# A router's mask and row weights moved from VectorE to GpSimd in a recurrence plus mixture-of-experts kernel

## The reference

```
d = sigmoid(x Wd + bd);  i = x Wi + bi;  h_t = d_t * h_(t-1) + i_t       # recurrence over the tokens
x = layernorm(x + (layernorm(h) * gamma + beta) + x)

gate = x Wg^T + routing_bias                                              # 8 experts
mask = the 4 largest of 8 (ties: the lower index first)
weights = softmax(gate where mask) * mask
ffn(u; w1, w2, w3) = (silu(u w1) * (u w2)) w3                             # hidden size 682
x = layernorm(x + ffn(x; shared) + sum over the 4 chosen experts of weight * ffn(x; expert))
```

## Time and profile before

| | us |
|---|---|
| three runs | 982.51, 984.04, 985.51 (median 984.04) |
| profiled execution | 981.17 |
| its span | 979.4 |
| PE busy | 960.3 (98%) |
| PEld busy | 785.1 (80%) |
| DVE busy | 560.8 (57%) |
| POOL busy | 554.8 (57%) |
| ACT busy | 504.7 (52%) |

### The profile page before, as it was taken

How to read it: one execution, slowest core, us unless ns; L and a number is a source line. 1 busy time by engine, 2 the same in 40 slices (tenths; PEclk the granted TensorE clock), 3 DMA queues, 4 the chain that set the end, 5 groups by cost and what they waited for, 6 DMA issues and landing times.

```text
span 979.4 us, 25637 instructions
## 1 busy us (share of the span) xinstructions
PE 960.3 (98%) x8131; PEld 785.1 (80%) x8131; DVE 560.8 (57%) x1410; ACT 504.7 (52%) x1259; POOL 554.8 (57%) x547
## 2 busy tenths in 40 slices
PE   9997999999999999999999999999999999999997
PEld 4554667788887888888788878788888887887885
DVE  4899977745554446544545445444454454544686
ACT  3666544445554455545455445444555554554366
POOL 4586047759433348534855035086898870885883
PEclk9999999999999999999999999999999999999999
DMA  6887124473532333533345214129754881795785
GB/s 224 248 167 172 28 70 125 101 212 101 160 104 89 98 100 94 158 109 101 92 103 135 59 39 145 46 54 198 119 94 85 125 123 49 110 131 88 101 153 143
DMA packets 168052, 113.88 MB, mean 116 GB/s; under 512 B 113596, under 2 KB 160191, under 8 KB 166848
## 3 DMA queue, kind: packets, MB, share of 16 engines
q0 software_dynamic: 29808, 58.37, 27.2%
q1 hardware_dynamic: 115888, 33.15, 16.8%
q10 hardware_dynamic: 22304, 21.76, 6.7%
HBM read 47.09 MB, written 43.12 MB: 92 GB/s over the span
## 4 chain that ended last, share of the span: by engine, by line
PE 80%; POOL 6%; DVE 5%; issue 3%; DMA 3%; ACT 1%; SPq 1%; ACTq 0%; DVEq 0%; POOLq 0%
PE psA L1161 50%; PE psB L1192 21%; PE psA L1090 5%; POOL y_sum L805 3%; DMA rows_by_place<-y_rows,place 2%; POOL rows_by_place L741 2%; PE psB L1195 2%; PE psA L1192 1%; DVE g_lo L1614 1%; PE psB L1103 1%; PE psC L1134 1%; DVE work L1380 0%; DMA y_sum<-rows_by_place,place 0%; DVE g L1604 0%; PE psC L1263 0%
## 5 line engine op out<-in xcount | busy, mean ns | idle before, releaser
L913 ACT ACTIVATE sil<-psA 128x256 f32<-128x256 f32 (+1 forms) x456 | 178.6, 399 | 273.8 <-PE psA L1161 237.1
L805 POOL DMA_INDIRECT y_sum<-rows_by_place,place x128 | 199.5, 1558 | 81.2 <-issue 37.8
L1604 DVE SCALAR_TENSOR_TENSOR g<-psA,sil 128x256 f32<-128x256 f32 (+1 forms) x160 | 71.9, 450 | 297.2 <-ACT sil L913 296.6
L1161 PE MATMUL psA<-xb_odd,work 128*128 128x256 f16 x1980 | 221.1, 273 | 0.2 <-issue 0.2
L1161 PEld LDWEIGHTS psA<-xb_odd,work 128*128 128x128 f16 x1980 | 193.5, 98 | 23.0 <-issue 0.6
L1192 PE MATMUL psB<-work,g_hi 128*128 128x256 f16 x1260 | 211.1, 273 | 0.0
L1161 PE MATMUL psA<-xb,work 128*128 128x256 f16 x1782 | 199.0, 273 | 2.2 <-issue 1.2
L1161 PEld LDWEIGHTS psA<-xb,work 128*128 128x128 f16 x1782 | 173.8, 98 | 24.0 <-issue 4.0
L1604 DVE SCALAR_TENSOR_TENSOR psC<-psA,sil 128x256 f32<-128x256 f32 (+3 forms) x296 | 133.0, 449 | 77.8 <-ACT sil L913 72.3
L752 POOL DMA_INDIRECT rows_by_place<-y_rows,place x96 | 95.0, 989 | 136.6 <-DMA rows_by_place<-y_rows,place 121.2
L1192 PE MATMUL psB<-work,g_lo 128*128 128x256 f16 x630 | 171.7, 273 | 0.0
(11 more groups left out here) (191 smaller groups left out, 1010.7 us busy)
## 6 DMA issues: line engine op xcount, KB each, us to landing
stage<-wpack POOLq DMA_DIRECT2D x9, 2176.0 KB, 9.1
rows_by_place<-eb ACTq DMA_DIRECT2D x57, 256.0 KB
work<-xT SPq DMA_DIRECT2D x7, 512.0 KB, 6.1
work<-half_beta SPq DMA_DIRECT2D x6, 512.0 KB, 5.7
work<-x_tok POOLq DMA_DIRECT2D x6, 512.0 KB, 6.0
rows_by_place<-eb ACTq DMA_DIRECT2D x6, 384.0 KB
rows_by_place<-zeros SPq DMA_DIRECT2D x1, 2112.0 KB, 13.5
rows_by_place<-y_rows,place POOLq DMA_INDIRECT x128, 2.5
```

The source lines that it names most:

```text
L805: pool.indirect_dma_start(out=y_sum[:, n, :], out_offset=None, in_=xs, in_offset=bass.IndirectOffsetOnAxis(ap=place[:, k, n:n + 1], axis=0 ...
L913: act.activation(sil[r0:r0 + n, c % SLOTS, 0:T], psA[0:n, chunk_bank(c, T), 0:T], ACT.Silu, scale=1.0 / (XS * WS)).then_inc(silu_ready, 1)
L1161: last = pe.matmul(dst, W[:, ws, k, ci, :], xb[slot][:, KD * xs_ + k, 0:T], start=(k == 0 and n == 0), stop=(k == KD - 1 and n == 2))
L1604: dve.scalar_tensor_tensor(gated_rows(g, c, 0, n, T), src, 1.0 / (XS * WS), sil[r0:r0 + n, c % SLOTS, 0:T], ALU.mult, ALU.mult).then_inc(g ...
```

## The change

It does these things:

- **Mask on POOL** (`choose`): difference of each logit from the fourth largest, of the four largest from it, equality and greater-than, running counts of the equal ones by three additions (ties), and from these the mask; in all sixteen operations behind the maxima, the first of which is the shift for the exponentials. DVE keeps the 32 maxima, now all behind the last logits, between the products of chunks 4 and 5 of block 0.
- **Row weights on POOL** (`weigh`): multiplication by the mask, sum of 8 in three additions, power of -0.5, square, scale, product.
- **Exponentials** on ACT ahead of block 1 instead of after it; the last step's normalisation goes beside the chunks of block 1.
- **Order on DVE**: low parts of rows beside chunks 1 and 2 of block 1, counts beside 3, place keys beside 4, half the key maxima beside 5 and half at the block's end. PE's rank product stands after chunk 2.
- **Order on PE** in the recurrence: states of the next step ahead of the second half of the products.
- **SP**: the zero fill is issued in step 6 instead of step 1.
- **PE's loop over pairs** is written out four times, with fixed pair words and constant waits.
- Two memsets of constants fall away.

```diff
@@ sync @@
-                if s == 1:
-                    fill_spare()
                 if s == EARLY - 2:
                     load_ahead(0)
+                if s == EARLY:
+                    fill_spare()
@@ gpsimd @@
+            def choose():
+                t = Tally(pool, route_steps)
+                fourth = top[:, :, K - 1:K]
+                equal, pair_sum, quad_sum = ties
+                pool.wait_ge(y_ready, NSTEP - 1)
+                for tie in ties:
+                    t.add(pool.memset(tie[:, :, 0:K], 0.0))
+                pool.wait_ge(largest_ready, 1)
+                pool.tensor_tensor(ex[:, :, :], gate[:, :, :], top[:, :, 0:1].to_broadcast([P, NT, E]), ALU.subtract)\
+                    .then_inc(shifted_ready, 1)
+                t.add(pool.tensor_tensor(over, gate[:, :, :], fourth.to_broadcast([P, NT, E]), ALU.subtract))
+                t.add(pool.tensor_tensor(fours, top[:, :, 0:K], fourth.to_broadcast([P, NT, K]), ALU.subtract))
+                t.wait()
+                t.add(pool.tensor_scalar(equal[:, :, K:TW], over, 0.0, 1.0, ALU.is_equal, ALU.mult))
+                t.add(pool.tensor_scalar(fours, fours, 0.0, 1.0, ALU.is_equal, ALU.mult))
+                t.wait()
+                t.add(pool.tensor_scalar(over, over, 0.0, 1.0, ALU.is_gt, ALU.mult))
+                t.add(pool.tensor_tensor(pair_sum[:, :, K:TW], equal[:, :, K:TW], equal[:, :, K - 1:TW - 1], ALU.add))
+                t.add(pool.tensor_tensor(twos, fours[:, :, 0:2], fours[:, :, 2:4], ALU.add))
+                t.wait()
+                t.add(pool.tensor_tensor(quad_sum[:, :, K:TW], pair_sum[:, :, K:TW], pair_sum[:, :, K - 2:TW - 2],
+                                         ALU.add))
+                t.add(pool.tensor_tensor(fours[:, :, 0:1], twos[:, :, 0:1], twos[:, :, 1:2], ALU.add))
+                t.wait()
+                t.add(pool.tensor_tensor(tie_rank, quad_sum[:, :, K:TW], quad_sum[:, :, 0:E], ALU.add))
+                t.wait()
+                t.add(pool.tensor_tensor(tie_rank, fours[:, :, 0:1].to_broadcast([P, NT, E]), tie_rank, ALU.subtract))
+                t.wait()
+                t.add(pool.tensor_scalar(tie_rank, tie_rank, 0.0, 1.0, ALU.is_ge, ALU.mult))
+                t.wait()
+                t.add(pool.tensor_tensor(tie_rank, tie_rank, equal[:, :, K:TW], ALU.mult))
+                t.wait()
+                pool.tensor_tensor(mask_h[:, :, :], tie_rank, over, ALU.add).then_inc(mask_ready, 1)
+            def weigh():
+                ...
+                t.add(pool.tensor_tensor(es_root[:, :], es[:, :], neg_half[:, 0:1].to_broadcast([P, NT]), ALU.pow))
+                ...
             pool.wait_ge(rows_marked, 8)
+            choose()
+            weigh()
@@ scalar @@
-            normed(NSTEP - 1)
+            act.wait_ge(shifted_ready, 1)
+            act.activation(ex[:, :, :], ex[:, :, :], ACT.Exp).then_inc(exps_ready, 1)
+            act.activation(nstat[0][:, 0, 0:2], bd, ACT.Silu).then_inc(table_loaded, 1)
+            act.wait_ge(table_loaded, 1)
...
-            ffn_block(1, TL)
-            act.wait_ge(shifted_ready, 1)
...
+            ffn_block(1, TL, beside=lambda c: normed_part(NSTEP - 1, c))
@@ tensor @@
                 turn_parts(s)
-                if s + AHEAD < NSTEP:
-                    products(s + AHEAD, [1])
...
                 if s + 1 < NSTEP:
                     states(s + 1)
+                if s + AHEAD < NSTEP:
+                    products(s + AHEAD, [1])
+                if s + 1 < NSTEP:
                     gate_sums(s + 1)
...
-            ffn_block(SH, 1, TL, early_slot(1), beside=lambda c: ranks() if c == 3 else None)
+            ffn_block(SH, 1, TL, early_slot(1), beside=lambda c: ranks() if c == 2 else None)
...
-            with pe.Fori(0, E // 2) as p:
-                counted(pe, weight_set_ready, 2 * p + 1)
-                expert_turns(0, lambda c: read_second(pair_words[0], c))
...
+            for p in range(E // 2):
+                pe.wait_ge(weight_set_ready, 2 * p + 1)
+                expert_turns(0, lambda c: read_second(pair_words[p], c))
+                pe.wait_ge(weight_set_ready, 2 * p + 2)
+                expert_turns(1, lambda c: read_first(pair_words[p + 1], c) if p + 1 < E // 2 else None)
@@ vector @@
             low_first(1)
             gated_first(3)
-            largest_early()
             low_first(2)
             gated_first(4)
+            largest()
             low_first(3)
             gated_first(5)
             low_first(4)
             low_first(5)
-            choose(0, EARLY_CHOSEN)
```

More of the change, by code:

```diff
@@ L166, in build @@
         seg = sb("seg", [P, E, NT], F32)
-        tot, inc = (work[:, 11, n * NT * E:(n + 1) * NT * E].rearrange("p (e t) -> p e t", e=E) for n in range(2))
-        key = work[:, 11, 2 * NT * E:3 * NT * E].rearrange("p (t e) -> p t e", e=E)
+        tot, inc = (work[:, 12, n * NT * E:(n + 1) * NT * E].rearrange("p (e t) -> p e t", e=E) for n in range(2))
+        key, over = (work[:, 12, n * NT * E:(n + 1) * NT * E].rearrange("p (t e) -> p t e", e=E) for n in (2, 3))
+        TW = K + E
+        ties = [work[:, w, n * NT * TW:(n + 1) * NT * TW].rearrange("p (t e) -> p t e", e=TW)
+                for w, n in ((10, 0), (10, 1), (12, 0))]
+        tie_rank = work[:, 12, NT * TW:NT * (TW + E)].rearrange("p (t e) -> p t e", e=E)
+        fours = work[:, 10, 2 * NT * TW:2 * NT * TW + NT * K].rearrange("p (t e) -> p t e", e=K)
+        twos = work[:, 10, 2 * NT * TW + NT * K:2 * NT * TW + NT * (K + 2)].rearrange("p (t e) -> p t e", e=2)
         place = sb("place", [P, K, NT], U32)
@@ L866, in acts, with normed_part, normed @@
                         .then_inc(products_read, 1)
-            def normed(s):
+            def normed_part(s, part):
                 b = s % B
                 g0 = tok(s) // P
-                act.wait_ge(rstd2_ready, s + 1)
-                for j in range(JT):
-                    last = act.activation(y[:, g0 + j, :], zr[b][:, j, :], ACT.Identity,
-                                          scale=rs2[b][:, j:j + 1], bias=nb2[b][:, j:j + 1])
-                last.then_inc(y_ready, 1)
-                act.wait_ge(y_ready, s + 1)
-                act.activation(y_hl[:, g0:g0 + JT, 0, :], y[:, g0:g0 + JT, :], ACT.Copy, scale=XS)\
-                    .then_inc(y_high_ready, 1)
+                if part == 0:
+                    act.wait_ge(rstd2_ready, s + 1)
+                if part < JT:
+                    last = act.activation(y[:, g0 + part, :], zr[b][:, part, :], ACT.Identity,
+                                          scale=rs2[b][:, part:part + 1], bias=nb2[b][:, part:part + 1])
+                    if part == JT - 1:
+                        last.then_inc(y_ready, 1)
+                else:
+                    act.wait_ge(y_ready, s + 1)
+                    act.activation(y_hl[:, g0:g0 + JT, 0, :], y[:, g0:g0 + JT, :], ACT.Copy, scale=XS)\
+                        .then_inc(y_high_ready, 1)
+            def normed(s):
+                for part in range(JT + 1):
+                    normed_part(s, part)
             def copy_sums(s):
@@ L995, in first_high @@
                     .then_inc(first_high_ready, 1)
-            ffn_block(1, TL)
-            act.wait_ge(shifted_ready, 1)
-            act.activation(ex[:, :, :], ex[:, :, :], ACT.Exp).then_inc(exps_ready, 1)
-            act.activation(nstat[0][:, 0, 0:2], bd, ACT.Silu).then_inc(table_loaded, 1)
-            act.wait_ge(table_loaded, 1)
+            ffn_block(1, TL, beside=lambda c: normed_part(NSTEP - 1, c))
             def first_high_beside(g):
@@ L1725, in _ @@
             low_first(5)
-            choose(0, EARLY_CHOSEN)
-            t.wait()
-            t = late
             add_shared(0, ahead_tiles(0))
```

109 lines of the change are left out of this document (37 added, 72 removed).

## The result

The changed kernel takes 988.9 us, median of 9 runs (987.46 to 995.08), the kernel before 984.04 (981.58 to 986.73, 9 runs on the same chip): ratio 1.0051, 95% interval 1.0031 to 1.0071. That is +4.9 us, where +2.1 was forecast; 988.9 lies above the forecast's own range (983.5 to 988.5) and inside the whole one (980 to 990). "Slower by over 0.3%" had a chance of 0.33.

A forecast was written before the change was run, and what follows sets the result against it. PE bounds the experts, so its arrival there sets the end. Recurrence -2.8, blocks 0 and 1 +6.0, pairs -0.8, hand-over -0.3 sum to +2.1 us: 986.1 on the median, own range 983.5 to 988.5, whole 980 to 990.

The forecast's parts named there:

- What bounds the kernel: PE is busy 687.73 of 690 us from 200 to 890, so whatever moves its arrival at the experts moves the end.
- Recurrence, -2.8: Steps 1 and 3: DVE's waits of 1.98 and 1.46 us shrink by PE's order and the later fill; -1.3 to -3.4.
- Blocks 0 and 1, +6.0: Late maxima, the mask on POOL and DVE's longer list at block 1's end hold PE: +6.0 us.
- three of the second (1.2): In the mask on POOL: three 256-element operations with one input, 0.41 us each, within an undisturbed 9.0 us.
- +3.2 of block 0: Block 0's down projection on PE ends at 106.7 instead of 103.47, held by late low parts and POOL's turns.
- Pairs, -0.8: Entry to the second pair of experts: written out, PE is spared the loop's return, 0.82 us of issue.
- Hand-over, -0.3: At the first expert PE's wait of 0.31 us for rows goes, as PE comes later than the rows.
- weights on POOL hold the port: Block 1's end: a 5.2 us power on POOL blocks DVE's counts' scan, 3.5 more, +5.6 in all, 989.6; chance 0.27.
- the port costs nothing: Blocks 0 and 1: the mask is in time, only DVE's list at block 1's end holds PE; -1.1, 982.9; chance 0.15.
- PE is not held at all: Blocks 0 and 1: low parts and mask come in time, so only gains are left, 979.8; chance 0.21.

The follow-up runs named there:

- fill_between: The kernel before with PE's new recurrence order and the zero fill behind the eighth norm and the loads of block 1's rows: 982.88 us, ratio 0.9980.
- pairs_loop: The changed kernel with PE's counted loop over the pairs put back: 987.17 us, ratio 1.0038 to the kernel before.
- pairs_only: The kernel before with only PE's four pairs of experts written out instead of a loop: 987.23 us, ratio 1.0033.
- maxima_last: pairs_loop with DVE's maxima behind block 0's last low part, rank products, counts and keys moved back with them: 987.04 us, ratio 1.0028 to the kernel before.
- keys_in_block2: pairs_loop with the place keys at block 1's end and both halves of their maxima in block 2: 986.24 us, ratio 1.0016 to the kernel before.

## Why the prediction was right, and where it was not

- **What bounds the kernel**: right. PE from 200 to 890 is busy 686.05 of 690 (before 687.73), and what moves its arrival moves the end, but for what the phase takes or gives. That making the router's way shorter "is worth 0.3 us at most" held only while PE was no earlier: 2.9 us earlier it is worth 2.05 (fill_between).
- **Recurrence, -2.8**: right as a size (-2.93, -2.94, -2.87, -2.92 in four kernels), but not in every run of the kernel as it stands. "It shares the engines with step 7's x, asked for some 10 us after its issue: 0 to +1, I take 0" failed: it is step 6's x that POOL asks for at the moment of the fill, and in the two traces where they meet within 0.6 us the price is 5.1. Most runs of the changed kernel seem to be spared it: -2.9, +5.5, +3.3 and -0.3 make +5.6 (an estimate from the kernels above), near the +4.9 of the median, while with the wait it would be some +10.8. The order alone gave +0.12: it needs the fill out of its way.
- **Blocks 0 and 1, +6.0**: right in size, 5.48 to 5.71 in the four kernels that have these edits, and right in its path (late maxima, late mask, then the lists at block 1's end), but partly by luck. The maxima, which follow the last logits (forecast near 97) at once, start at 98.25 in pairs_loop, 97.15 on before's clock. Block 0's down projection waits 2.24 (3.2), the rank product 1.83 in the changed kernel (1.9). The mask itself, 12.4 forecast and 11.55 measured, came out by two errors against each other: "three of the second (1.2)" are comparisons and take 1.10, 1.08 and 1.08 undisturbed, so that the undisturbed mask is about 10.7 instead of 9.0, and the disturbance by DVE is some 0.8 instead of 3.4. The +3.2 of block 0 is no cost of its own either: the wait for the mask holds PE to the same moment.
- **Pairs, -0.8**: the failed step. Alone the edit costs +3.3 (+1.1 to +5.3), and undoing it in the changed kernel moves the ratio from 1.0051 to 1.0038, with overlapping intervals. I had "0 if new code must be fetched as slowly" as the worst end; the wait is 2.25 to 2.32 in three kernels, against 0.67 to 0.82 with the loop. The term is off by 4.1 us alone and by some 2 in the changed kernel; the gap between forecast and result is 2.8. The Trainium skill, in "Runtime: NRT & Kernel Launch", section "Instruction fetch mechanics", says that a branch taken out of the window makes an engine fetch before it goes on, and that kernels therefore prefer unrolling; here the loop's turn cost less than entering new code. The instruction queue moved 0.59 MB in place of 0.33; that the wait is for this fetch is likely and not shown, since the profile names no releaser for it.
- **Hand-over, -0.3**: right, no wait at the first expert.
- **Rival "weights on POOL hold the port"**: its price was right (5.45 for 5.2), its consequence refuted: DVE's two-input operations ran at their usual length inside it. The rule that I had cited for it, in the Trainium skill's "SBUF — State Buffer", section "SBUF: two separate sides" (the one that starts first keeps the pair for its whole instruction), fits the 1.53 us subtractions as far as a low part that starts inside one goes, not the power; the trace decides.
- **Rival "the port costs nothing"**: refuted by the stretched low parts and mask operations, but nearer than I had it: the price on PE's path is about the 0.8 us by which the mask is later (an estimate). That the mask would be "there before PE asks" with the port free was wrong by the comparisons: at 10.7 us it ends near 113, where 111.45 was asked.
- **Rival "PE is not held at all"** did not come true, but the order for it exists: it decides where the maxima, the rank products and the counts stand, not three us earlier logits, as I had put it.
- **Not foreseen**: the experts' 0 to 2.9 us by phase.

Open stay why a transfer that starts 0.6 us before the fill is delayed by 5 us and one 1.6 us before not at all, and the rest of pairs_only's loss.

## What to carry to other kernels

Moving work off an engine that is not the bound wins nothing where it stood in cover; what counts is which instruction is now first in line behind a late input. Put the operation that waits for another engine behind everything the bound is waiting for, and the product that consumes it as late as its consumer allows. A wait of the bound engine costs nothing of its own when a later wait would have held it to the same moment; price the chain that ends last, not each wait. Before timing small edits ahead of a long steady stage, look whether that stage has a beat between two engines: its phase can hide or fake 0.3%.

## What the runs showed of the hardware

- After its 5.52 us wait (90.38) PE was granted half its clock, and the 36 matmuls behind it took 8.19 us (36 of the same take 6.01 at 103.17 in fill_between, at full clock). The windows of the changed kernel (start:end, length, busy by engine, clock, DMA share, GB/s):

```profile
88.00:94.00 6.00, 3.62 (x12) 1.76 (x13) 5.47 (x12) 3.07 (x6) 4.65 (x10) 0.50 0.85 157
```

- Behind a wait of 2.38 us it fell too (maxima_last, where the six matmuls behind it took 2.13 us instead of 1.15):

```profile
114.00:118.00 4.00, 3.81 (x18) 2.37 (x19) 2.85 (x9) 1.00 (x2) 3.54 (x6) 0.58 0.05 10
```

- The same wait does not always do it. Behind 1.65 and 0.41 us in block 0 the clock was 0.50 in pairs_loop and 1.00 in keys_in_block2; behind 2.28 us in pairs_only it stayed at 1.00:

```profile
104.00:106.00 2.00, 2.00 (x10) 1.20 (x8) 0.85 (x3) 1.89 (x3) 1.92 (x4) 0.50 0.00 0
104.00:106.00 2.00, 2.00 (x15) 1.22 (x13) 0.64 (x2) 1.43 (x4) 1.92 (x4) 1.00 0.00 0
446.00:452.00 6.00, 6.00 (x57) 5.39 (x56) 2.69 (x7) 2.71 (x9) 1.92 (x2) 1.00 0.14 48
```

- DVE's low part that reads one input from PSUM was not held by POOL (0.41 at 467.64 in the changed kernel, inside a POOL subtraction from 467.62); those that read both from SBUF were, in the experts one chunk in three.
- On POOL a comparison costs more than a product of the same shape: 1.08 us against 0.41 for 128x256 f32.
- A POOL power goes by the element even when it is short: 0.72 and 1.02 for 2 and 4 per partition, 5.45 for 32.
